# The turned maxima of both attentions are laid into the query rows by ACT's queue, behind the copy of the sums

## What is computed

```python
scores = jnp.einsum('bhqd,bhkd->bhqk', q, k) / jnp.sqrt(jnp.float32(D_K))
probs = jax.nn.softmax(scores, axis=-1)
out = jnp.einsum('bhqk,bhkd->bhqd', probs, v)
...
x = x + _L0_xattn_ref(_layernorm(x, axis=-1), ctx_1024, ctx_1024, ...)
x = x + _L0_ffn_ref(_layernorm(x, axis=-1), ...)
x = x + _L1_xattn_ref(_layernorm(x, axis=-1), ctx_1024, ctx_1024, mask_BxS2_if1, ...)   # causal
x = x + _L1_ffn_ref(_layernorm(x, axis=-1), ...)
```

## Time and profile before

| What | Value |
|---|---|
| median of 3 runs (lowest, highest) | 437.22 (437.04, 439.81) |
| the profiled execution's own time | 438.72 |
| its span in the trace | 437.0 |
| mean granted TensorE clock | 0.931 |
| busy of the span: PE, DVE, ACT, POOL | 82%, 66%, 51%, 21% |
| attention of layer 0, about | 39 to 137 |
| attention of layer 1, about | 279.7 to 386 |

### The profile page before, as it was taken

How to read it: one execution, slowest core, us unless ns; L and a number is a source line. 1 busy time by engine, 2 the same in 40 slices (tenths; PEclk the granted TensorE clock), 3 DMA queues, 4 the chain that set the end, 5 groups by cost and what they waited for, 6 DMA issues and landing times. The chain is left out here.

```text
span 437.0 us, 10507 instructions
## 1 busy us (share of the span) xinstructions
PE 356.5 (82%) x3434; PEld 256.6 (59%) x3434; DVE 288.8 (66%) x905; ACT 224.7 (51%) x420; POOL 89.9 (21%) x163
## 2 busy tenths in 40 slices
PE   1484677888977999999999999789899999757663
PEld 0352556766763567776677767557677676534442
DVE  5675677988965753574433443696789899367893
ACT  2142345656664664444434343146566656648894
POOL 6335040020203002100101001124333342310000
PEclk9887599999998999999999999889999999856997
DMA  7555864334317000650161100103444331000111
GB/s 200 119 145 126 209 162 129 118 113 119 97 30 240 2 1 5 127 111 1 35 179 41 36 0 0 37 14 108 132 124 113 96 103 29 3 1 1 32 30 37
DMA packets 54100, 34.98 MB, mean 80 GB/s; under 512 B 38744, under 2 KB 46256, under 8 KB 54064
## 3 DMA queue, kind: packets, MB, share of 16 engines
q1 hardware_dynamic: 44032, 31.43, 26.7%
q10 hardware_dynamic: 10032, 3.08, 3.0%
HBM read 24.60 MB, written 9.44 MB: 78 GB/s over the span
## 5 line engine op out<-in xcount | busy, mean ns | idle before, releaser
L1039 ACT ACTIVATE probs<-ps_e 128x512 f32<-128x512 f32 x128 | 75.5, 594 | 60.7 <-PE ps_e L884 55.9
L957 DVE TENSOR_REDUCE neg<-ps_s 128x4 f32<-128x512 f32 x128 | 85.2, 685 | 23.3 <-PE ps_s L867 22.1
L1285 DVE SCALAR_TENSOR_TENSOR x_all<-ps_ym,c_g,x_all 128x128 f32 (+1 forms) x128 | 36.0, 344 | 63.1 <-PE ps_ym L1380 63.0
L1380 PEld LDWEIGHTS ps_ym<-w,hid 128*128 128x128 f32 x512 | 60.8, 192 | 9.2 <-issue 6.7
L1380 PE MATMUL ps_ym<-w,hid 128*128 128x128 f32 x512 | 62.2, 276 | 0.0
L1370 PE MATMUL ps_h<-tok_t,w 128*128 (+1 forms) x128 | 61.9, 607 | 0.0
L1487 ACT ACTIVATE hid<-ps_h,b 128x512 f32<-128x512 f32 x64 | 43.1, 684 | 35.3 <-PE ps_h L1370 33.9
L867 PE MATMUL ps_s<-k_rows,q_rows 96*128 96x128 bf16 x512 | 54.0, 233 | 8.7 <-PEq L448 3.9
L884 PE MATMUL ps_e<-q_rows,k_rows 128*128 128x128 bf16 x512 | 50.6, 224 | 11.0 <-DMA q_rows<-neg_t 10.3
L867 PEld LDWEIGHTS ps_s<-k_rows,q_rows 96*128 96x128 bf16 x512 | 40.1, 104 | 22.2 <-issue 9.6
L884 PEld LDWEIGHTS ps_e<-q_rows,k_rows 128*128 128x128 bf16 x512 | 36.2, 100 | 17.7 <-DMA q_rows<-neg_t 10.1
(11 more groups left out here) (200 smaller groups left out, 552.5 us busy)
## 6 DMA issues: line engine op xcount, KB each, us to landing
k_rows<-k_dram SPq DMA_DIRECT2D x32, 144.0 KB
q_rows<-q_dram SPq DMA_DIRECT2D x32, 144.0 KB
k_rows<-k_dram SPq DMA_DIRECT2D x16, 288.0 KB
q_rows<-q_dram SPq DMA_DIRECT2D x16, 288.0 KB
k_dram<-parts SPq DMA_DIRECT2D x35, 128.0 KB, 2.3
w<-in_w SPq DMA_DIRECT2D x16, 128.0 KB, 2.6
q_dram<-parts SPq DMA_DIRECT2D x15, 128.0 KB, 2.2
q_dram<-parts ACTq DMA_DIRECT2D x9, 128.0 KB, 3.1
```

The source lines that it names most:

```text
L957: dve.tensor_reduce(neg[:, s, q * HQ:(q + 1) * HQ], ps_s[:, q % 2, :].rearrange("p (h k) -> p h k", h=HQ), AX_X, ALU.max, negate=True).the ...
L1039: act.activation(probs[:, s, q, :], ps_e[:, q % 2, :], ACT.Exp, scale=SCALE).then_inc(exp_done, 1)
L1285: dve.scalar_tensor_tensor(out=batch_of(x_all, g * G + j), in0=ps_y[:, e % 2, j * D:(j + 1) * D], scalar=c_g[:, j, e:e + 1], in1=batch_of( ...
L1380: last = pe.matmul(ps_y[:, e % 2, j * D:(j + 1) * D], hid[:, (e % 2) * M + m, j * P:(j + 1) * P], w2[:, e, m, :], start=(m == 0), stop=(m ...
```

## The change

`lay_maxima` moves from SP to ACT. On SP it goes from the end of each `load`, from the start (batches 0 and 1) and from the end (batches 14 and 15). On ACT it stands at q = 0 behind `copy_maxima(b + 1)` and `copy_sums(b - 1)`, with the same wait for `negt_ready`, so that ACT's sequencer waits for ACT's own copy. The transfer, its destination and its semaphores are the same. On SP the stores and weights that stood behind a lay now stand behind a load.

```diff
         @block.sync
-            def lay_maxima(b, r):
-                wait(sp, negt_ready, b + 1)
-                sp.dma_start(q_rows[ROW_MAX:ROW_MAX + PARTS, r], neg_t[:, r % 2, :]).then_inc(neg_laid[r], 16)
             def load(b, r):
...
-                lay_maxima(b - 2, (r - 2) % SLOTS)
...
-            for b in range(2):
-                lay_maxima(b, b)
-                if layer == 0 and b == 1:
-                    store_unit(sp, c, LATE[3], c["last_stored"])
+            if layer == 0:
+                store_unit(sp, c, LATE[3], c["last_stored"])
...
-            for b in range(B - 2, B):
-                lay_maxima(b, b % SLOTS)
...
         @block.scalar
+            def lay_maxima(b, r):
+                wait(act, negt_ready, b + 1)
+                act.dma_start(q_rows[ROW_MAX:ROW_MAX + PARTS, r], neg_t[:, r % 2, :]).then_inc(neg_laid[r], 16)
...
                     if q == 0 and exists(b - 1):
                         copy_sums(b - 1, 1 - s)
+                    if q == 0 and exists(b + 1):
+                        lay_maxima(b + 1, (r + 1) % SLOTS)
                     if q == 1 and exists(b - 2):
                         copy_output(b - 2, s)
```

## The result

| | before | changed |
|---|---|---|
| median (lowest to highest, runs) | 438.51 (437.04 to 439.95, 4) | 447.46 (446.89 to 448.77, 4) |
| ratio, with its 95% interval | | 1.0223 [1.0187, 1.0259] |
| the same file in a later comparison, median | 437.87 (433.19 to 440.50, 23) | 444.84 (441.59 to 447.38, 6) |
| ratio there | | 1.0164 [1.0127, 1.0201] |
| profiled execution: span, mean granted clock | 437.0, 0.931 | 447.1, 0.917 |

The change costs 7 to 9 us. The forecast was 438.9 with a range to 443.5; both medians lie above it. The ratios leave out the few executions in the chip's slower state (461.85 in e6, at a granted clock of 0.807; 439.82 and 440.50 among those of before in the later comparison).

A forecast was written before the change was run, and what follows sets the result against it. The prediction took the projection, at the end of a chain on ACT, to bound both layers. Layer 0's -0.7 and layer 1's +2.4 made +1.7 on 437.22, thus 438.9, range 432.4 to 443.5.

The forecast's parts named there:

- What bounds the kernel: Both layers: the projection ends a chain of copies and an exp on ACT, with no spare time worth naming.
- The issue: On ACT: the transfer takes 0.70, starting +0.30 after the maxima's copy starts; exp of q = 1 then starts at +1.09.
- each 0.1 costs 2.5: Exp of q = 1 on ACT: between +1.09 and the late-issue case's +1.55, each 0.1 later costs 2.5.
- a late start of the issue alone: Rival on ACT: the issue waits for the copy of the sums, exp starts at +1.55; +13.1, 450.3; chance 0.10.
- The ten steady steps: Layer 0's ten steps: 51.1 against 50.47, +0.6, as the projection comes 0.44 later in each.
- The two steps ahead of them: Layer 0, the two steps before the steady ones: prompt lays win 1.3 and 0.6, together -1.9.
- The start: Layer 0's first lays, batches 0 and 1: taken as 0, bounds 0.9 won and 0.7 lost.
- the start goes wrong: Rival at layer 0's start: the first two lays land 2 to 3 late behind ACT's stores; +2.5, 441.4; chance 0.12.
- The end: Layer 0's batches 14 and 15: DVE bounds one step, the projection the other; +0.6 (0 to 0.9).
- Layer 1: Ten steps at 0.20 and three at 0.46 make 3.4, less 0.8 absorbed from mask-row waits; rounded, +2.4 (0.5 to 4.8).
- The sum: Whole kernel: layer 0's -0.7 plus layer 1's +2.4 gives +1.7, median 438.9.

The follow-up runs named there:

- e6: The changed kernel with ACT's lay moved to q = 1, behind the copy of the output: 438.98, ratio 1.0035 to the kernel before.
- e5: The kernel before, SP's lay kept, plus a same-form transfer on ACT at the change's place into a buffer nobody reads: 447.05, ratio 1.0226.
- e11: The changed kernel with ACT's steps of both attentions written out in place of the loop: 443.08, ratio 1.0120 to the kernel before.
- e7: The changed kernel run once more, unedited: 444.84, ratio 1.0164 to the kernel before.
- e9: The kernel before, with SP's lay in layer 0 placed between the two halves of a load: 437.42, ratio 0.9989.
- e3: The changed kernel, but SP lays batches 0 and 1 of layer 0, with its stores behind them: 443.81, ratio 1.0130 to the kernel before.
- e4: The kernel before, with both layers' lays issued by POOL's queue behind its fill of v_aug, which then waits for the copied maxima: 446.73, ratio 1.0181.
- e2: The kernel before, with only layer 1's maxima laid by ACT and layer 0's still by SP: 441.36, ratio 1.0062.
- e1: The kernel before, with only layer 0's maxima laid by ACT and layer 1's still by SP: 441.11, ratio 1.0079.
- e12: The kernel before, lay still on SP, with ACT's steps of both attentions written out in place of the loop: 436.98, ratio 1.0000.

## Why the prediction was wrong

**What bounds the kernel: right.** That "the projection sits at the end of a chain on ACT in both layers" and "has no spare time worth naming" is what e5 and e6 show from both sides: the delay without the lay costs everything, the lay without the delay nearly nothing. In layer 0 the waits for the lay and the late projection cover each other in part (e5), as the forecast had it.

**The issue: right in size and start, short behind it.** 0.70 was 0.73; the start at +0.30 held in every step. The gap of 0.09 behind an issue was taken from one place in straight code. In the changed kernel it is 0.10 in straight code too, but 0.18 in the steps of the loop. The exp thus starts at +1.13 in straight code and at about +1.22 in the loop, in place of the +1.09 of the forecast. e11 moves it to +1.13. The text had said that "each 0.1 costs 2.5", and that the kernel is slower by over 1% from a start of about +1.2 on, and tied that case to a late start of the issue alone. This is the first step that failed: a slope was worked out, and its input was read to 0.01 from a single pair of rows in straight code. The second is the start, below.

**The ten steady steps: the term mis-sized.** Forecast +0.6, measured +2.1 (e7) to +2.3 against before. The rule used there was a projection, then 3.10 to the next copy, or 3.25 with pieces of DVE's. In e7 the ten projections stand at +1.94 to +2.06, 20.1 in sum. The rest, 52.59 - 20.1 = 32.5, is what the rule gives (2 x 3.10 + 8 x 3.25 = 32.2). With 1.89 in each of the ten steps the forecast had 18.9. So 1.2 of the missing 1.5 is the late exp. The rule holds only where the projection is the last to be late: in e9 the ten projections stand at 16.8 in sum, the rule gives 49.0, and 50.81 was measured.

**The two steps ahead of them: right**, -1.9 against -1.94 in e7. In the first profile after, the low clock hid it. The DVE CAST ended behind POOL's addition again (60.78 to 62.92, the addition from 58.35 to 62.90). The Trainium skill ("SBUF — State Buffer", "Who interferes with whom") would have it so, and the trace agrees.

**The start: put at nothing, and the rival came true in one of its two lays.** The forecast took 0 and gave 12% to "the start goes wrong" with +2.5. The first lay gained 0.8, the second was late: 4.30 from issue to PE (2.18 in before), with 1.79 of waiting where there had been none. The stage lost 1.4 against before's profile and 2.1 against the mean of three, 0.7 of it clock. e5 takes the issue out of suspicion (11.37 with two issues on ACT), e3 has part of the loss back with the same two lays on SP. The forecast weighed only what stands in ACT's queue. It left out that SP, freed of its lays, issues its five stores about 6 us earlier, beside ACT's five (46.11 for both, before 52.08), and that the second lay goes out right behind them. Its working for the second lay was one sentence without a price.

Whether the place behind ACT's own stores or the load of both queues' stores makes it late stays open; e4 has a wait of 1.81 with no store in its own queue, but from a slower one. The Trainium skill ("DMA: Bandwidth & Descriptors", "Queues, rings and completion order") says that each ring is served in its order, and the lay behind the stores agrees with it. The forecast had cited this very rule, for the first lay only.

**The end: not contradicted.** The forecast was +0.6. The means have +0.4, but the stage with the experts scatters by 2.4 between profiles of the lay on SP (165.24 to 167.68), so it isn't sized.

**Layer 1: mechanism right, size short.** Forecast +2.4; +2.3 to +3.3 in profiles against before's, +3.5 in the means, +3.3 in e2's median. The forecast's own terms, 3.4 less 0.8, make 2.6; the 0.2 taken off "with rounding" has no row. The exp at +1.22 in place of +1.09 makes 0.13 more in the loop's eight steps, and +1.13 makes 0.04 more in the five others, 1.2 in all. That is enough for the difference, and e11's 13 steps, 0.75 under the others' mean, bear out the loop's part of it.

**The sum** of small terms of both signs hid that each was uncertain by its own size. With the late exp (+1.2 and +1.2) and the start at +2.1 the same working gives 1.7 + 4.5 = +6.2, what the stages and e1 and e2 show. All three errors had the same sign. The range had room for just that: +6.3 is its very top, worked out there from an issue of 0.82 and a small loss at the start; the measured medians are 0.7 to 2.7 above it. The clock drop took 2.4 of the profiled execution; of the other three in that median there is no profile.

## What to carry to other kernels

An issue is work of the engine that makes it: 0.73 on ACT for this transfer, plus what stands behind it in the instruction stream. Before moving a transfer to an engine, find the waits of that engine and put the issue ahead of one (ahead of an exp that PE has yet to feed it cost 0.35%, ahead of a copy that PE waits for 1.6 to 2.2%). A wait that a move removes is worth nothing until the next late thing is known; here PE's 4.7 of waits for the lay were covered by those for DVE and the projection. And look at what the queue that is relieved will do: here SP's stores went out about 6 us earlier and met ACT's, and the one small transfer that PE waited for came late among them.

## What the runs showed that was not expected

- Behind an issue on ACT the next exp starts 0.10 later in straight code and 0.18 later in the loop. Writing ACT's steps out moved it from +1.22 to +1.13; where no issue stood, it moved only four exps of layer 1, by 0.08, and the time not at all (e12, ratio 1.0000).
- An issue can start while the exp ahead of it on the same engine runs: in e6 at +0.75 beside an exp from +0.65 to +1.23, and the copy of the output then started at +1.13, inside the issue's 0.73. In the changed kernel the exp waited for the issue's end (103.93 to 104.11). So the copy that had stood ahead in the program wasn't held up, and the one behind was.
- Taking SP's lays away moved SP's stores from 52.08 to 46.11. The share of the DMA engines from copy 1 to copy 2 rose from 0.64 to 0.96, and PE waited 1.79 there for a lay that had cost it next to nothing.
- The granted clock fell to half for 6.8 us in one profile of layer 0's attention and not in the other profile of the same file; this one stretch moved a step by 2.4, a third of the whole effect.
- Layer 1 with an unchanged attention took 85.80 to 89.09 in five profiles. Its first two steps took 10.0 in most, and 11.2 to 12.1 in e3, e6, e9 and e11, where the clock from copy 17 to 18 was 0.69 to 0.76 and not 1.00. The 13 steps behind them stayed within 1.3 of each other. To size a term of 1, cut such steps off, or compare several kernels that share the code.
